# Local layer: half-phase softmax and weighted sum moved across the phase border, score blocks and rotations reordered

## The reference

```python
for i in range(DEPTH):                                  # 6
    x = attn_layer(shift_tokens(x), Wqkv[i], q_scale[i], k_scale[i], Wo[i]) + x
    x = ffn_layer(shift_tokens(x), ln_g[i], ln_b[i], W1[i], b1[i], W2[i], b2[i]) + x

def attn_layer(x, Wqkv, qs, ksc, Wo):
    q, k, v = heads of x @ Wqkv                         # 16 heads of 64
    q = l2norm(q) * qs;  k = l2norm(k) * ksc
    q, k = rotary positions (cos, sin) on q and k
    out = local_attention(q, k, v)                      # windows of 32, each sees itself and the one before
    return out @ Wo

def ffn_layer(x, g, bln, W1, b1, W2, b2):
    hg = layernorm(x) @ W1 + b1
    a, gate = jnp.split(hg, 2, -1)
    return a * gelu(gate) @ W2 + b2
```

## Time and profile before

| | |
|---|---|
| time of 3 runs, median (lowest to highest) | 9550.41 us (9549.36 to 9557.72) |
| profiled execution: its own time | 9542.88 us |
| profiled execution: span | 9541.1 us |
| loop of the local layer, 23 whole turns of 24 | 3694.2 us |
| PE busy in that loop | 3224.7 us |
| DVE busy in that loop | 2784.7 us |

### The profile page before, as it was taken

One profiled execution on the slowest core, in us unless ns is written; L12 is line 12 of the kernel. 1 busy time (PEld: TensorE's weight loads), 2 busy tenths in 40 slices (PEclk: granted clock), 3 DMA queues, 4 the chain that ended last, 5 costly groups with the idle time before them and its releaser, 6 DMA issues. The chain is left out here.

```text
span 9541.1 us, 245537 instructions
## 1 busy us (share of the span) xinstructions
PE 7287.1 (76%) x92569; PEld 4453.7 (47%) x92569; DVE 6764.2 (71%) x15000; ACT 3257.0 (34%) x5970; POOL 3224.7 (34%) x3982
## 2 busy tenths in 40 slices
PE   4888888888874826656845768888888888888887
PEld 3666666666621212223223345545455545454554
DVE  7777777777758475765485557777777777777776
ACT  2222222222243313223413334444444444444444
POOL 1333333333300000210040035555555555555553
PEclk7888888888887867656865779999999999999999
DMA  0000000000000000000000031111111111111111
GB/s 18 1 1 1 1 1 1 1 1 1 1 5 1 15 0 0 0 0 1 0 0 1 1 120 54 53 53 54 48 56 51 54 51 51 56 51 56 51 56 57
DMA packets 156976, 243.21 MB, mean 25 GB/s; under 512 B 21617, under 2 KB 136849, under 8 KB 150161
## 3 DMA queue, kind: packets, MB, share of 16 engines
q1 hardware_dynamic: 155920, 228.84, 7.8%
HBM read 187.06 MB, written 13.66 MB: 21 GB/s over the span
## 5 line engine op out<-in xcount | busy, mean ns | idle before, releaser
L2751 POOL TENSOR_TENSOR big<-big 128x512 f32<-128x512 f32 x776 | 1040.1, 1373 | 278.4 <-DMA big<-norms 270.7
L2741 POOL TENSOR_TENSOR big<-big 128x512 f32<-128x512 f32 x388 | 494.7, 1275 | 1819.8 <-DVE big L2583 1819.8
L882 POOL TENSOR_TENSOR big<-big 128x128 f32<-128x128 f32 x1024 | 518.3, 506 | 1569.7 <-DVE big L820 1567.4
L604 ACT ACTIVATE big<-big 128x128 f32<-128x128 f32 x1024 | 316.8, 309 | 1902.0 <-DVE big L778 1876.8
L1856 POOL TENSOR_TENSOR small<-big 128x480 f32<-128x480 f32 (+14 forms) x240 | 220.9, 954 | 2187.2 <-ACT big L1614 1866.5
L2158 PE MATMUL banks<-hidden,big 128*128 128x256 f32 x3104 | 828.9, 401 | 111.8 <-DVE big L2583 41.1
L514 PE MATMUL banks<-big,constants_on_chip 128*128 128x128 f32 x2048 | 533.3, 347 | 409.8 <-DVE big L811 408.2
L337 PE MATMUL banks<-big,constants_on_chip 128*128 128x512 f32 (+15 forms) x1088 | 533.5, 644 | 355.2 <-DVE big L1747 191.3
L337 PE MATMUL banks<-big,weights_even 128*128 128x512 f32 (+5 forms) x1152 | 620.5, 692 | 235.0 <-DVE big L1137 45.1
L2222 PE MATMUL banks<-big,hidden 128*32 128x512 f32 x6144 | 770.5, 600 | 4.1 <-ACT big L2473 4.1
L2201 PEld LDWEIGHTS banks<-big 32*32 32x32 f32 x49152 | 535.2, 103 | 471.8 <-issue 471.1
(11 more groups left out here) (349 smaller groups left out, 15896.3 us busy)
## 6 DMA issues: line engine op xcount, KB each, us to landing
big<-norms SPq DMA_DIRECT2D x776, 128.0 KB, 2.9
big<-qk SPq DMA_DIRECT2D x50, 512.0 KB, 4.8
big<-vo SPq DMA_DIRECT2D x25, 1024.0 KB, 5.8
weights_odd<-ffn SPq DMA_DIRECT2D x25, 537.5 KB, 4.6
hidden<-big SPq DMA_DIRECT2D x171, 64.0 KB, 12.9
hidden<-big SPq DMA_DIRECT2D x25, 256.0 KB, 3.8
hidden<-big SPq DMA_DIRECT2D x25, 255.8 KB, 4.0
big<-pairs SPq DMA_DIRECT2D x6, 1024.0 KB, 10.4
```

Of the source, the lines that this page charges most:

```text
L882: nc.gpsimd.tensor_tensor(full(u["kS"][s % 2]), full(S), by(u["ko_c"]), ALU.mult).then_inc(*e.did(("kS", s)))
L2741: self.nc.gpsimd.tensor_tensor(dst, cos, sin, ALU.add).then_inc(*e.did(("turned_pair", f, name, g)))
L2751: self.nc.gpsimd.tensor_tensor(x, x, u["norms"][:, n, g].unsqueeze(1).broadcast_to([P, 2, QTOK]), ALU.mult).then_inc(*e.did(("scaled", f, ...
```

## The change

Every engine's list inside a phase is written in another order; no matmul, activation or vector instruction of the loop is added or dropped.

- The second half's `exps` and `normalise` (jj = 1) leave the end of phase f and stand in phase f + 1, behind the first square and the first key rotation. `attend(f, 1)` was in phase f + 1 already and now stands behind K3; in phases 1 to 3 the first two `value` groups stand ahead of it.
- The first score block of a phase stands right behind that sum (in phase 0 ahead of it), before the sums of keys and the query projections.
- `normalise(f, 0)` moves up between the rotations of Q1 and Q2, `lower(f, 0)` between Q0 and Q1; `lower(f, 1)` is DVE's last attention step.
- The second half's score masks and first score move ahead of Q2 and Q3. `mean` and `centre` go from the end of phase 0 into phase 1. The values of phase 3's second half, made early before, are now made late as in the other phases, so the `vo` load comes later too.
- The loop's entry clears `slots` and `prob[1]` in place of `probT[1]`; the exit does the last `exps` and `normalise`.

```diff
@@ local_tensor
             for g in range(3):
                 t.project(f, "K", g)
-            t.attend((f - 1) % QUARTERS, 1)
+            if f:
+                t.value(f, 0, 0)
+                t.value(f, 0, 1)
             t.project(f, "K", 3)
-            t.value(f, 0, 0)
-            t.value(f, 0, 1)
-            t.sums(f, "K")
-            t.project(f, "Q", 0)
+            if f:
+                t.attend((f - 1) % QUARTERS, 1)
             t.score_masks(f, 0)
             t.score(f, 0, 0)
+            if f == 0:
+                t.attend((f - 1) % QUARTERS, 1)
+                t.value(f, 0, 0)
+                t.value(f, 0, 1)
+            t.turn_back(f)
+            if f == 1:
+                t.mean(0)
+            t.score(f, 0, 1)
+            t.sums(f, "K")
+            t.score(f, 0, 2)
+            t.project(f, "Q", 0)
+            if f == 1:
+                t.mean(1)
+            t.score(f, 0, 3)
+            t.value(f, 0, 2)
             t.project(f, "Q", 1)
-            t.score(f, 0, 1)
-            t.turn_back(f)
+            t.value(f, 0, 3)
+            t.score_masks(f, 1)
+            t.score(f, 1, 0)
             t.project(f, "Q", 2)
-            t.score(f, 0, 2)
             t.project(f, "Q", 3)
-            t.score(f, 0, 3)
+            t.value(f, 1, 0)
+            t.score(f, 1, 1)
             t.sums(f, "Q")
...
@@ local_scalar
-            for g in range(GROUPS):
-                a.square(f, "K", g)
-            a.keep_value(f, 0, 0)
-            a.keep_value(f, 0, 1)
-            a.square(f, "Q", 0)
+            a.square(f, "K", 0)
+            a.exps((f - 1) % QUARTERS, 1)
+            a.square(f, "K", 1)
+            a.square(f, "K", 2)
...
@@ local_vector
-            for name in NAMES:
-                for g in range(GROUPS):
-                    v.rope(f, name, g)
-                v.guard(f, name)
-            v.lower(f, 0)
+            v.rope(f, "K", 0)
+            v.normalise((f - 1) % QUARTERS, 1)
+            for g in range(1, GROUPS):
+                v.rope(f, "K", g)
             v.add(f, (turn % BATCH) * SEQ + (f - 1) * QTOK if f else old + 3 * QTOK)
             if f == 1:
+                v.centre(0)
+            v.guard(f, "K")
+            v.rope(f, "Q", 0)
+            if f == 1:
+                v.centre(1)
+            v.lower(f, 0)
+            v.rope(f, "Q", 1)
+            v.normalise(f, 0)
+            v.guard(f, "Q")
+            v.rope(f, "Q", 2)
+            v.rope(f, "Q", 3)
+            if f == 1:
                 v.norm(0)
-            if f >= 2:
-                v.gate(f - 2, 0)
-            v.normalise(f, 0)
-            if f == 1:
                 v.norm(1)
             if f >= 2:
-                v.gate(f - 2, 1)
-                v.gate(f - 2, 2)
+                for k in range(len(IC)):
+                    v.gate(f - 2, k)
             v.lower(f, 1)
-            if f == 0:
-                v.centre(0)
-                v.centre(1)
             if f >= 2:
                 v.ffn_add(f - 2, old)
-            v.normalise(f, 1)
```

More of the change, by code:

```diff
@@ L2228, in attend @@
         e, pe, u = self.e, self.pe, self.u
+        pe.wait_ge(*e.after("turned", q, jj))
         if e.layer == "local":
-            kw = {"back": 1} if jj and q == QUARTERS - 1 else {}
-            pe.wait_ge(*e.after("turned", q, jj, **kw))
-            pe.wait_ge(*e.after("kept", q, jj, 3, **kw))
+            pe.wait_ge(*e.after("kept", q, jj, 3, **({"back": 1} if jj and q == QUARTERS - 1 else {})))
             if jj == 0:
@@ L2363, in entry_vector @@
         e.name_last("folded", d, "vector")
+    for k in range(2 * (SUBS * QUARTERS) - 5, 2 * (SUBS * QUARTERS)):
+        nc.vector.memset(u["slots"][k % SLOTS], 0.0).then_inc(*e.did())
+    dve.wait_ge(*e.after("stored", DEPTH - 1))
+    nc.vector.memset(u["prob"][1].rearrange("p c k -> p (c k)"), 0.0).then_inc(*e.did())
     e.leave()
@@ L2459, in exps @@
         e, act = self.e, self.act
-        act.wait_ge(*e.after("lowered", f, jj))
+        if e.layer == "local":
+            act.wait_ge(*e.after("lowered", f, jj, **({"back": 1} if jj and f == QUARTERS - 1 else {})))
         p = self.u["prob"][jj].rearrange("p c k -> p (c k)")
@@ L2622, in normalise @@
         self.chain()
-        if jj:
-            dve.wait_ge(*e.after("attended", (f - 1) % QUARTERS, 1))
-        else:
-            pf, kw = earlier(f)
-            dve.wait_ge(*e.after("attended", pf, 0, **kw))
+        if e.layer == "local":
+            pf, kw = earlier(f if jj == 0 else (f + 1) % QUARTERS)
+            dve.wait_ge(*e.after("attended", pf if jj == 0 else (f - 1) % QUARTERS, jj, **kw))
         self.nc.vector.transpose(u["probT"][jj].rearrange("p c w q -> p (c w q)").bitcast(U32),
@@ L2811, in exit_scalar @@
     for h in range(HALVES):
-        a.gelus(h, range(3))
+        a.gelus(h)
     core.to_act.restart("out")
```

86 lines of the change are left out of this document (45 added, 41 removed).

## The result

The changed kernel takes **9721.3 us** (median of 4 runs, 9717.89 to 9729.4) beside 9554.06 for the kernel before (4 runs, 9549.36 to 9563.18): a ratio of **1.0175, interval 1.0157 to 1.0193**. It is slower, as forecast, but by 167 us where the forecast was 62, and it lies outside the range. The profiled execution took 9723.93 us.

The account below looks back on a forecast made before the run. The prediction saw the loss in PE's waits for softmax transposes and instructions late behind the `vo` load. A walked 157.9 us plus 5.3 of extras gave 163.2 a turn, 2.6 more, times 24: 9612 us median, range 9500 to 9690.

Parts of the forecast that it names:

- The walk over the changed order: Step-by-step schedule of PE and DVE through the four changed phases, priced from the profile, undisturbed: 157.9 us a turn.
- the same walk before: The same priced schedule for the old order, without slow clock or late instructions: 153.4 us a turn.
- The first sign named for a wrong prediction: Second half's masks on PE: forecast to wait for the lowering, about 1.2 us a phase; no wait would refute it.
- PE's late instructions: Profile sign: these waits without a visible releaser leave phase 3's scores and show at the turn's start.
- What comes on top: Extras beyond the walk per turn, 7.2 us before: late instructions 2.0, slow clock 1.8, DVE against POOL 1.5, together 5.3.
- Slow clock: PE work at 1.2 GHz in place of 2.4 after waits: taken 1.8 us a turn, about 2 before.
- The wait of 4.79 has gone and 2.31 can pass at full clock: Waits before PE's sums at starts of phases 2 and 1: claim behind taking slow clock at 1.8 us.
- Late instructions: Instructions delayed behind the 1 MB `vo` load, now around the turn's jump: taken 2.0 us a turn, 3.6 before.
- DVE against POOL: DVE's division slowed beside POOL's scaling of keys in all four phases, half hidden: taken 1.5 us a turn.
- The jump under the load: Rival: all engines' first instructions of a turn wait for the `vo` load, slow sums follow; 9730 us, chance 0.12.
- Faster: Rival: load hides under PE's wait at the turn's start, no sum at slow clock; 9517 us, chance 0.26.

Follow-up runs that it names:

- a_softmax_late: Changed kernel with first half's softmax and query-sum clamp behind Q3's rotation, its sum behind the last values, last score and values before third `up`: 0.5% faster than before.
- a_vo_small: Changed kernel with the loop's `vo` load cut to 128 of its 2048 columns: 0.8 us a turn less than the changed kernel.
- a_vo_early: Changed kernel with phase 3's last two values, and so the `vo` load, about 11 us earlier: 3.55 us a turn less than the changed kernel.
- a_shift: Changed kernel with one DVE clear in the entry cut into 32, moving DVE's loop 31 instructions on: 1.1 us a turn less than the changed kernel.
- b_vo_small: Kernel before with the loop's `vo` load cut to 128 of its 2048 columns: 0.5% less time by ratio, turn 0.2 us shorter.
- a_pairs: Changed kernel with first half's last two and second half's first two values next to each other again: turn 0.3 us shorter, ratio 0.4% under the changed kernel's.
- b_border_in: Kernel before with second half's softmax behind the next phase's K0 rotation, values and K3 before its sum, only at starts of phases 1 to 3: 1.1% faster.
- a_jump_vo: Changed kernel with the old softmax and sum order at the turn's jump, and phase 3's values and `vo` load early: level with the kernel before.
- a_jump_kept: Changed kernel with softmax and sum of phase 3's second half around the turn's jump as before: 3.5 us a turn less, 1.2% by the ratios.
- c_pe_shift: b_border_in with each of the entry's 96 matmuls done twice, so PE's loop stands further on: 1.3 us a turn longer (159.0), ratio 0.6% up.
- b_border: Kernel before with second half's softmax behind the next K0 rotation, values and K3 ahead of its sum, at all four borders: 0.3% slower than before.
- a_lower_first: Changed kernel with the first half's lowering ahead of Q0's rotation on DVE: 1% slower than the changed kernel.
- a_masks_late: Changed kernel with the second half's masks and first score behind Q2: 1.4 us a turn less than the changed kernel, 0.6% by the ratios.
- d_all_masks: a_softmax_late with the turn's jump as before, phase 3's values early, and second half's masks and first score behind Q2: 9448 us, 1.3% below the kernel before.

## Why the prediction was wrong in size

**Right:** the direction and its mechanism. The walk over the changed order gave 157.9 us with nothing disturbed, 4.5 more than the same walk before. Its waits are in the trace: sums 8.0 a turn (8.9 forecast), masks 3.7 (4.5), banks of variance and `up` 5.1 (4.5 to 5). The first sign named for a wrong prediction, masks that do not wait, did not come. a_softmax_late takes the banks' waits away by undoing the moves that the walk blamed for them. Of the signs named, PE's late instructions did not go to the turn's start alone: 1.4 us a turn came up in phase 2's scores.

**The step that failed is "What comes on top".** The prediction let the extras fall from 7.2 to 5.3 us a turn; they rose to 168.0 less 157.9 = 10.1. That is an error of 4.8 us a turn, all of the distance between the 2.6 forecast and the 7.4 measured. Term by term:

- *Slow clock, taken 1.8 (bounds 0.5 and 4).* The long steps are 5.7 a turn; with the same count they were 4.2 before, not the "about 2" that I read from single sums. I looked at sums alone. Masks and scores behind a wait are slow too (0.8 and 0.9 us a turn), and the wait of K3 at the jump, 3.56 where it was 1.52, makes K3 slow as well. The granted clock is at its lower level for 8.6 us of a turn before and 14.1 after. "The wait of 4.79 has gone and 2.31 can pass at full clock" was wrong: in the turn shown a wait of 2.24 was followed by a sum of 2.87 at 0.68. The term was 3.9 us too small. Part of that was too small before as well and cancels: the term was to fall by 0.2 and rose by 1.5, which is 1.7 of the 4.8.
- *Late instructions, taken 2.0 (bounds 0 and 5.2).* PE has 1.4 a turn left in phase 2's scores, and K3's wait in phase 0 is 3.56 where the walk had 1.6 (K0's rotation until 4.5, PE through at 2.85): together 3.3, 0.3 under the 3.6 where the forecast was 1.6 under: 1.3 of the 4.8. About 1.0 of it is the load (a_vo_small, a_vo_early) and about 1.1 to 1.3 the gap in the rotation (a_shift). I had seen neither the gap, which before was not there, nor that 2.6 of the old 3.6 had nothing to do with the load (b_vo_small).
- *The rest,* 1.8 of the 4.8. PE's turn is its idle time and its steps: idle rose by 3.1 (20.4 to 23.5), steps by 4.3 (140.2 to 144.5), of them 1.5 long steps and 1.6 in the values (30.2 to 31.8), now partly alone between other shapes; a_pairs takes 1.0 of these back. The walk priced a value alone at 1.0, so it had this in part. And the walk before was itself too long: long steps of 4.2 and late instructions of 4.2 (3.6 before scores) make 8.4, over the 7.2 that it left for everything on top.
- *DVE against POOL, taken 1.5.* No run changes it alone. The division takes 1.33 us in the mean before, 1.41 after (eight a turn, so 0.6 us) and 1.62 in a_softmax_late, which is the faster kernel; so it does not make the change slow.

**The rivals.** *The jump under the load* gave 9730, close to the 9721 measured, but by another way: it had 5.2 us a turn of late landing where the runs show 1 (the load has 2.1 us left when `ffn_add` ends, and DVE's wait does not follow its landing), and what it took for slow sums was nearer. That it came out within 10 us is luck. *Faster* fell by its own condition, extras under 2.7.

**Where the 7.4 us come from,** by kernels that differ in one part of the change each; the last numbers are the same steps by the ratios, in us a turn:

```
before             160.6
b_border_in        157.7   -2.9  border part at the starts of phases 1 to 3     -4.3
a_jump_vo          162.4   +4.7  order inside the phases                        +4.1
a_jump_kept        164.5   +2.2  phase 3's last values and the vo load late     +2.4
after              168.0   +3.5  border part at the turn's jump                 +4.7
```

Signs and order hold by both, the sizes within 1.4 us. In the second step PE's late instructions fall from 4.4 to 1.6 us a turn, so what else the order does comes to some 7.5; where they fall also depends on where the loop stands (c_pe_shift), and no step was repeated with a shift. The sum is in this order only. Taken in another order the parts differ (the early load gives 3.6 from the changed kernel, 2.2 with the jump kept, nothing once the softmax is late), which fits one chain: a late rotation makes PE wait, that wait slows PE's next groups, DVE enters the next phase late, and the load leaves late. What is shown is that all of it goes when the first half's softmax, the clamp and the sum no longer stand ahead of Q2 and Q3 and of the last score: undone together (a_softmax_late) they give the 7.4 back and 0.4 more. How much of this is the softmax on DVE and how much the order on PE is not shown. Why that is more than the 5.1 us of bank waits is shown in part (K3 -2.0, long steps -1.3, sums +1.6); which of them follow from which I have not separated.

## What to carry to other kernels

Before a wait is shortened by putting work ahead of a long vector operation, list what then stands behind that operation on its engine: here 4.3 us of softmax stood in front of two rotations whose banks PE needed. That made 5.1 us a turn of waits for banks, more than the 3.6 that the sums' waits gave back, and moving it away with its clamp and sum was worth 7.8. Price the border at a loop's jump apart from those inside, for there the engine's own wait for its first input and the jump are part of the chain: the same move gained 3.4 us at the inner borders and lost 5.5 at the jump (b_border). And count the slow clock over all groups behind a wait, in the kernel before too, not over the group that the wait is named after.

## What the runs showed of the hardware

- Late instructions depend on where the loop stands in the stream: 31 more DVE instructions ahead of it took a gap of 1.3 us a turn away, and more PE instructions ahead of PE's loop made its gaps 5.6 us a turn from 4.4. Two orders of the same work can differ by over 1 us a turn of 160 for this reason alone. One shift was tried on each engine.
- A 1 MB load in flight while DVE jumps delayed DVE's first instruction behind the jump by 1.0 us (3.4 in place of 2.4), the same whether it landed 1.6 or 3.4 us into that wait.
- PE fell to the lower clock (0.68 and 0.55 granted over the sum and what follows) behind waits of 2.24 and 2.91 us, and the group after the first was slow too: masks of 0.61 us took 1.03. The lower level held for 8.6 us of a turn before, 14.1 after, 24.3 in a_lower_first.
- Removing waits one by one did not add up: with the masks' wait gone (3.7 us a turn) the kernel got slower by 4.5 us a turn in one order (a_lower_first), and with most of it gone faster by 1.4 and 2.1 in others (a_masks_late, d_all_masks).
